# One core, attention block and experts: the output projection between queries and keys, attention's sums in two halves, and three smaller moves

## What is computed

```python
def _L0_attn_ref(q_x, ...):                      # H = 16 heads of HD = 16
    xn = _ln(q_x, ln1_w, ln1_b)
    q = (xn @ wq + bq).reshape(b, n, H, HD).transpose(0, 2, 1, 3)          # k and v likewise
    fq = jax.nn.elu(q) + 1.0
    fk = jax.nn.elu(k) + 1.0
    kv = jnp.einsum('bhnd,bhne->bnde', fk, v)    # a sum over the heads of each token
    qkv = jnp.einsum('bhnd,bnde->bhne', fq, kv)
    k_sum = fk.sum(axis=1)
    qk = jnp.einsum('bhnd,bnd->bhn', fq, k_sum)
    attn = qkv / (qk[..., None] + 1e-06)
    attn = attn.transpose(0, 2, 1, 3).reshape(b, n, c)
    attn = attn @ wo + bo
    x = q_x + attn
    h = _ln(x, ln2_w, ln2_b)
    h = jax.nn.gelu(h @ fc_w + fc_b, approximate=False)
    return x + (h @ proj_w + proj_b)
def _L0_ffn_ref(x, ...):                         # the best K = 2 of 8 experts per sequence
    pooled = x.mean(axis=1)
    logits = pooled @ gate_w.T + gate_b
    ...
    expert_out = jax.nn.gelu(jnp.einsum('bsd,eod->beso', x, expert_w) + expert_b[None, :, None, :], approximate=False)
    return jnp.einsum('be,beso->bso', gates, expert_out)
x = x + _L0_attn_ref(_layernorm(x, axis=-1), ...)
x = x + _L0_ffn_ref(_layernorm(x, axis=-1), ...)
```

## Time and profile before

| | us |
|---|---|
| median of 3 runs | 1235.26 (1235.08 to 1236.95) |
| profiled execution, its own time | 1239.31 |
| its span, first to last instruction | 1237.5 |
| TensorE busy | 1073.0, 87% of the span |
| VectorE busy | 772.0, 62% |
| ScalarE busy | 528.7, 43% |
| GpSimd busy | 190.0, 15% |
| mean granted TensorE clock | 0.907 of full |

### The profile page before, as it was taken

The page is one execution under the profiler, slowest core; times in us unless marked ns, Lnnn a source line. Parts: engine busy times, 40 slices in busy tenths (PEclk is TensorE's granted clock), DMA queues, the critical chain, the costliest instruction groups (busy, mean ns, idle before and its releaser), DMA issues.

```text
span 1237.5 us, 21621 instructions
## 1 busy us (share of the span) xinstructions
PE 1073.0 (87%) x7112; PEld 792.3 (64%) x7112; DVE 772.0 (62%) x1692; ACT 528.7 (43%) x835; POOL 190.0 (15%) x113
## 2 busy tenths in 40 slices
...
DMA packets 242509, 170.06 MB, mean 137 GB/s; under 512 B 177040, under 2 KB 218256, under 8 KB 240144
## 3 DMA queue, kind: packets, MB, share of 16 engines
...
...
## 4 chain that ended last, share of the span: by engine, by line
PE 56%; DVE 16%; issue 9%; DMA 9%; ACT 7%; SPq 1%; POOL 1%; DVEq 1%; ACTq 0%; POOLq 0%
PE pq L963 13%; PE pj L949 10%; PE ps L926 9%; PE pq L871 7%; PE pt L935 5%; DMA nd<-scratch_nd 4%; DMA scratch_nd<-ot 4%; DVE nd L728 3%; DVE am L701 3%; PE pq L908 2%; DVE acc L819 2%; PE ps L1006 2%; PE ps L908 2%; PE pj L1052 2%; PE pt L908 1%
## 5 line engine op out<-in xcount | busy, mean ns | idle before, releaser
L717 DVE TENSOR_TENSOR hidden<-xhT,hidden 128x512 fp32r<-128x512 f32 x128 | 104.0, 812 | 215.2 <-ACT hidden L542 215.1
L541 ACT ACTIVATE xhT<-pq,col 128x512 f32<-128x512 f32 x128 | 88.0, 688 | 333.2 <-PE pq L963 332.9
L963 PE MATMUL pq<-hT,w_fc 128*128 128x512 f32 x768 | 220.3, 426 | 4.9 <-issue 3.1
L949 PE MATMUL pj<-w_pj,hidden 128*128 128x256 f32 x1536 | 213.4, 288 | 2.7 <-DVE hidden L717 2.7
L949 PEld LDWEIGHTS pj<-w_pj,hidden 128*128 128x128 f32 x1536 | 190.8, 188 | 17.3 <-DVE hidden L717 3.7
L926 PE MATMUL ps<-kq 48*128 48x128 f32 x1024 | 155.2, 434 | 35.1 <-DVE am L701 18.5
L926 PEld LDWEIGHTS ps<-kq 48*128 48x128 f32 x1024 | 133.8, 329 | 76.2 <-issue 47.6
L701 DVE TENSOR_TENSOR am<-ps,mask 128x512 f32<-128x512 f32 x256 | 163.9, 681 | 22.3 <-PE ps L926 21.5
L963 PEld LDWEIGHTS pq<-hT,w_fc 128*128 128x128 f32 x768 | 146.6, 204 | 35.2 <-issue 4.8
L871 PE MATMUL pq<-zT,w_e 128*128 (+1 forms) x256 | 116.8, 605 | 9.6 <-DMA b_e<-in_eb 7.3
L458 POOL TENSOR_TENSOR rs<-var,mhalf 128x4 f32<-128x4 f32 x16 | 18.5, 1159 | 559.3 <-DVE var L745 559.3
...
## 6 DMA issues: line engine op xcount, KB each, us to landing
...
scratch_q<-hidden SPq DMA_DIRECT2D x32, 512.0 KB, 4.6
scratch_k<-hidden SPq DMA_DIRECT2D x32, 512.0 KB, 6.1
scratch_nd<-ot SPq DMA_DIRECT2D x16, 1024.0 KB, 3.9
...
x_sb<-in_x SPq DMA_DIRECT2D x16, 512.0 KB, 4.7
scratch_v<-feat_v ACTq DMA_DIRECT2D x16, 512.0 KB, 2.8
```

Source lines behind the costliest of these rows:

```text
L541: nc.scalar.activation(gelub[:, u], pq[u][:, :], ACT.Gelu, bias=b_fc[:, m:m + 1])
L717: nc.vector.tensor_tensor(hidden[:, m % SLOTS, 1], gelub[:, u], hidden[:, m % SLOTS, 0].bitcast(f32), ALU.subtract).then_inc(S["rest_ready ...
L949: last = nc.tensor.matmul(pj[u][:, D * s:D * (s + 1)], hidden[:, m % SLOTS, a, lo:lo + P], w_pj[:, b, m], start=(m == 0 and n == 0 and s = ...
L963: last = nc.tensor.matmul(pq[m % 2][:, :], w_fc[:, b, c, P * m:P * (m + 1)], hT[:, a, c], start=(n == 0), stop=(n == len(order) - 1))
```

## The change

1. **D2 is split.** D2 now holds v and q, and the new stage **D4** holds k. The order is `D2, A2, R, D4, K1, F1, F3, ...` instead of `D2, K1, A2, F1, R, F3, ...`. q goes into the `pt` banks, k into the `pq` banks that held v (`qk_bank`). Rounding of q and k is no longer interleaved with the exponentials. R writes its result to `xhat`, since `hn` holds k's features then.
2. **Sums in two halves.** SyncE stores and reloads the first 64 of each 128 tokens' sums in M2, and the other 64 in M4. VectorE divides the first half in the new stage **N0** after M4, the second in N.
3. **F2 before B9** on TensorE, with the addition in the new stage **FA** behind B9, and **F4 before B0** on VectorE.
4. **GpSimd**: Y's two adds move to **YB** behind JA, R's add to **SA** behind F4.

The diff, cut to its core:

```diff
-FULL = [..., "M3", "Z", "D1", "M4", "XL", "X", "J7", "JA", "E", "VT", "N", "D2", "K1", "A2",
-        "F1", "R", "F3", "B0", "F4", "H", "FX", "B9", "F2"]
+FULL = [..., "M3", "Z", "D1", "M4", "N0", "XL", "X", "J7", "JA", "YB", "E", "VT", "N", "D2", "A2",
+        "R", "D4", "K1", "F1", "F3", "F4", "SA", "B0", "H", "FX", "F2", "B9", "FA"]
...
         def qk_bank(j):
-            return (ps[j], f"ps_full{j}") if j < NC else (pt[j - NC], f"pt_full{j - NC}")
+            return (pt[j], f"pt_full{j}") if j < NC else (pq[j - NC], f"pq_full{j - NC}")
...
-                if p.stage in ("B4", "M4"):
+                if p.stage in ("B2", "M2", "B4", "M4"):
+                    half = int(p.stage[1]) // 2 - 1
+                    part = slice(HALF * half, HALF * (half + 1))
                     wait("pt_free0", at("pt_free0"))
                     wait("pt_free1", at("pt_free1", 1))
-                    sp.dma_start(nd_dram.rearrange("j e h t -> (j e) (h t)"), ot[:, :, :].rearrange("p h t -> p (h t)")
-                                 ).then_inc(S["nd_out"], 16)
+                    sp.dma_start(nd_dram.rearrange("j e h t -> (j e) h t")[:, :, part], ot[:, :, part]).then_inc(S["nd_out"], 16)
                     wait("attnT_ready", at("attnT_ready"))
                     wait("nd_out", at("nd_out", 16))
                     for c, dst in ((0, num[:, 0]), (1, num[:, 1]), (2, den)):
                         src = nd_dram[:, P // H * c:P // H * (c + 1)].rearrange("j e h t -> (e h) j t")
-                        sp.dma_start(dst.rearrange("p (j t) -> p j t", j=NQ), src).then_inc(S["num_in"], 16)
+                        sp.dma_start(dst.rearrange("p (j t) -> p j t", j=NQ)[:, :, part], src[:, :, part]).then_inc(S[f"num_in{half}"], 16)
...
-                if p.stage == "Y":
-                    wait("y_ready", at("y_ready", 1))
+                if p.stage == "YB":
+                    wait("y_ready", at("y_ready"))
+                    for u in range(2):
+                        wait(f"pj_free{u}", at(f"pj_free{u}"))
                     nc.gpsimd.tensor_tensor(x1[:, :, :], x1[:, :, :], rows_of(0), ALU.add).then_inc(S["yb_ready"], 1)
...
-                if p.stage == "R":
+                if p.stage == "SA":
                     slot = x_sb[:, p.t % XRING]
-                    wait("h_ready", at("h_ready", 1))
+                    wait("h_ready", at("h_ready"))
+                    wait("acc_ready", at("acc_ready"))
...
-                if p.stage == "D2":
+                if p.stage in ("D2", "D4"):
+                    lo = 0 if p.stage == "D2" else NC
+                    for j in range(lo, lo + NC):
...
+                def divided(half):
+                    def part(tile):
+                        return tile.rearrange("p c (j b t) -> p c j b t", j=NQ, b=2)[:, :, :, half]
+                    d = part(nd[:, NC:NC + 1])[:, 0]
+                    wait(f"num_in{half}", at(f"num_in{half}"))
+                    link(nc.vector.reciprocal(d, d))
+                    for c in range(NC):
+                        n = part(num)[:, c]
+                        last = nc.vector.tensor_tensor(n, n, d, ALU.mult)
+                    link(last)
+                if p.stage == "N0":
+                    divided(0)
                 if p.stage == "N":
-                    wait("num_in", at("num_in"))
-                    link(nc.vector.reciprocal(den, den))
-                    link(nc.vector.tensor_tensor(num, num, den.unsqueeze(1).broadcast_to([P, NC, T]), ALU.mult))
+                    divided(1)
                     link(nc.vector.tensor_copy(attnT[:, 0], num))
...
-                    normed(hn, x1, lambda s: mv[:, s, 0:1], lambda s: rs[:, s:s + 1]).then_inc(S["h_ready"], 1)
+                    normed(xhat, x1, lambda s: mv[:, s, 0:1], lambda s: rs[:, s:s + 1]).then_inc(S["h_ready"], 1)
...
-                    for j in (4, 5, 0, 1, 2, 3):
+                if p.stage in ("D2", "D4"):
+                    for j in (4, 5, 0, 1) if p.stage == "D2" else (2, 3):
```

More of the change, by code:

```diff
@@ L157, in loop @@
         base = plus(at, rate, hi - lo)
-    first = ["L", "DS", "D1", "X", "D2"]
+    first = ["L", "DS", "D1", "X", "D2", "D4"]
     second = ["K0", "K1", "VL", "VT", "B0", "B9"]
     late = ["XS", "J2", "Z", "E"]
-    last = ["XL", "F1", "F3", "F4", "FX", "F2"]
+    last = ["XL", "F1", "F3", "F4", "FX", "F2", "FA"]
     def without(names, *out):
@@ L349, in run @@
                     sp.dma_start(out_sb[:, :, :], x2_dram[p.t]).then_inc(S["x2_in"], 16)
-                if p.stage == "D2":
-                    for n, c in enumerate("qk"):
-                        for m in range(NC):
-                            wait("lo_ready", at("lo_ready", NC * n + m + 1))
-                            sp.dma_start(qk_dram[n][p.t % 2].rearrange("w u (c p) t -> c p (w u) t", p=P)[m],
-                                         hidden[:, NC * n + m].bitcast(f32).rearrange("p w (u t) -> p (w u) t", t=HALF)
-                                         ).then_inc(S[f"{c}_out"], 16)
+                if p.stage in ("D2", "D4"):
+                    n, c = (0, "q") if p.stage == "D2" else (1, "k")
+                    for m in range(NC):
+                        wait("lo_ready", at("lo_ready", m + 1))
+                        sp.dma_start(qk_dram[n][p.t % 2].rearrange("w u (c p) t -> c p (w u) t", p=P)[m],
+                                     hidden[:, NC * n + m].bitcast(f32).rearrange("p w (u t) -> p (w u) t", t=HALF)
+                                     ).then_inc(S[f"{c}_out"], 16)
                 if p.stage == "VL":
@@ L502, in run @@
                     wait("am_used", at("am_used"))
[L504 to L509 removed]
+                if p.stage in ("D2", "D4"):
+                    lo = 0 if p.stage == "D2" else NC
+                    for j in range(lo, lo + NC):
                         bank, full = qk_bank(j)
                         wait(full, at(full, 1))
[L512 removed]
+                        wait("f_ready", at("f_ready"))
                         nc.scalar.activation(expb[:, j % 2], bank[:, :], ACT.Exp, bias=b_qkv[:, j:j + 1])
@@ L515, in run @@
                                              bias=b_qkv[:, j:j + 1]).then_inc(S[full.replace("full", "free")], 1)
-                        if j:
-                            rounded(j - 1)
-                    rounded(2 * NC - 1)
+                    for j in range(lo, lo + NC):
+                        wait("f_ready", at("f_ready", j - lo + 1))
+                        nc.scalar.activation(hidden[:, j, 0], (fq, fk)[j // NC][:, j % NC], ACT.Identity).then_inc(S["hi_ready"], 1)
                 if p.stage == "VT":
@@ L679, in run @@
                         nc.vector.tensor_tensor(w[:, 1], w32, w[:, 0].bitcast(f32), ALU.subtract).then_inc(split_done, 1)
-                if p.stage == "D2":
-                    def rest(j):
-                        wait("hi_ready", at("hi_ready", j + 1))
-                        src = (fq, fk)[j // NC][:, j % NC]
-                        nc.vector.tensor_tensor(hidden[:, j, 1], src, hidden[:, j, 0].bitcast(f32),
-                                                ALU.subtract).then_inc(S["lo_ready"], 1)
-                    for j in range(2 * NC):
+                if p.stage in ("D2", "D4"):
+                    lo = 0 if p.stage == "D2" else NC
+                    for j in range(lo, lo + NC):
                         _, full = qk_bank(j)
```

73 lines of the change are left out of this document (35 added, 38 removed).

## The result

Before 1235.17 us (1233.54 to 1236.95, 4 runs), changed 1270.88 us (1266.98 to 1275.95, 4 runs): ratio 1.0292, 95% interval 1.026 to 1.0325. The profiled executions took 1239.31 and 1268.08 us (spans 1237.5 and 1266.3), 28.8 us apart. What follows explains the 28.8. The forecast, 1241.0 us, was 30 us too low, and the time lies outside its range.

The account below looks back on a forecast made before the run. It took TensorE's own work to set the pace in iterations with experts, with idle time at the ends and half-clock stretches. Terms 9.6 + 5.7 + 0 - 6.5 - 3 = +5.8 us on the median 1235.26 gave 1241.0; range 1225 to 1255.

Parts of the forecast that it names:

- When A2 can start: Output projection in full iterations: YB's adds delay N's products, so TensorE idles 1.3 us before A2, bounds 0 to 2.5.
- The halves' 2.1 us: VectorE's N: with half the sums divided early, the remaining reciprocal and products are shorter, 2.1 us saved.
- The transfers gain nothing: Stores and reloads of sums: halves land at the same time as before, bounds 1.5 us earlier and 1 us later.
- The experts behind the keys: Between F1 and F3: F3 starts 9.65 us after A2's end, leaving TensorE idle 2.75 us; before it was 0.26.
- What is saved behind F3: F3 to M1 in full iterations takes 8.45 us without waits; net +1.6 us each, +9.6 in six.
- HEAD iterations: The three iterations with gates: the gates' work gives N time to finish for A2; +1.9 us each, +5.7 together.
- Iterations 2 to 6: Iterations without experts: k fills the time behind A2 but K1's data is late; 0 for five, bounds -1.9 to +2 each.
- The end: Iterations 16 and 17: A2 starts earlier and F2's wait for GpSimd goes; together -6.5 us, bounds -3 to -10.
- The clock: TensorE's clock may stay high around second scores but fall during F3; -3 us for both, range -17 to +20.
- The rule weighed: GpSimd adds hold VectorE instructions with two SBUF sources; by the skill's rule one-source ones could be held too.
- rival 4: Slower by more: A2 1.7 us later in 11 iterations, 1259; or clock falls before every F3, 1256. Chance 0.1 together.
- rivals, 2: Faster: the clock stays at 2.4 GHz into M1 and the gap before F3 does not lower it; 1226 us, chance 0.2.

Follow-up runs that it names:

- e13: The changed kernel with D4 and K1 put ahead of A2 again, nothing else; 1207.04 us, ratio 0.9791.
- e10: The kernel of e6 with N0 right ahead of N, so both halves are divided together; 1196.47 us, ratio 0.9698.
- e14: The changed kernel with R put behind D4 and K1, A2 still ahead of k; 1225.47 us, ratio 0.9934.
- e5: The changed kernel with YB's adds back right behind Y and SA's add also waiting for k's rests; 1247.64 us, ratio 1.012.
- e7: The kernel of e5 with R put behind D4 and K1, A2 still ahead of k; 1200.14 us, ratio 0.9723.
- e12: The kernel of e6 with YB behind JA, where the change has it; 1207.99 us, ratio 0.9788.
- e6: The kernel of e5 with D4 and K1 put ahead of A2 again; 1197.46 us, ratio 0.9701.
- e4: The kernel before with YB's two GpSimd adds alone moved behind JA; 1239.49 us, ratio 1.0037.
- e3: The changed kernel with SA's GpSimd add also waiting for k's rests, which changes only iterations 2 to 6; 1260.76 us, ratio 1.0204.

## Why the prediction was wrong

By e13 the change splits in two. The move of the output projection costs +0.3 at the start, +13.7 in 3 to 6, +16.6 with gates, +30.0 in full iterations, -0.9 at the end: 60 us. Everything else gives -7.1, -4.0, +9.4, -23.1, -6.4: -31 us. I had both signs and neither size.

1. **"When A2 can start."** Right in full iterations: waits of 1.35 to 1.95 us against 1.3, because N's products wait for YB. The halves' 2.1 us are no gain there, since A2's start hangs on GpSimd's end or F3 on its own chain (read from the rows; e10 shows it only where k covers N). At the end the early division gave 1.0 and 0.5. "The transfers gain nothing" was wrong, and item 5 has the price.
2. **"The experts behind the keys."** Right in every step: F3 at E + 9.4 instead of E + 9.65, idle 2.38 instead of 2.75. With R behind k's roundings the wait falls to 1.23 (e14; from 3.44 to 1.24 between e5 and e7), so R's place makes half to two thirds of it. Full iterations lose 14.0 us more in e14 than in e13, 13.5 of it idle time.
3. **"What is saved behind F3."** F4, H and F2 run without a wait, as said. F3 to M1 took 902.95 - 893.44 = 9.5 us, not 8.45: F3 itself 1.9 more, at half clock, and F2 0.6 less, at the full one. The forecast net of +9.6 with the clock's -3 is +6.6; measured +6.9. This is luck, agreement of a sum and not of its terms. Over the six iterations the part behind the mark Q grew by 16.5 us, not 12.3, and the part ahead of it shrank by 9.6, not 2.7. Without the move the other edits save 23.1 us there (11.5 less idle time, half-clock time 35.4 to 2.2 us, worth at most 16.6), and the move takes 30.0 (idle 20.2, half clock 16.4 us, worth at most 8.2).
4. **"HEAD iterations", +1.9 each: the step that failed.** Measured 11.5, 7.6 and 6.9, 26.0 instead of 5.7, which is most of the miss. Counted by the mark Q, the part ahead of it, which I took to shrink by 0.2 each, grew by 8.3, 3.0 and 3.3 us; the part behind it grew by 3.2, 4.7 and 3.6, not 2.1. I let the gates' work cover YB and N, and did not ask what YB stands in front of: the copies pb<-gs. TensorE waits 4.28, 4.28 and 3.88 us for them instead of 1.7, and is at half clock for 6.8 us around that in each, where before has 3.4, 3.4 and nothing. e12 against e6 prices this at 7.0, e13 against before at 9.4 with the rest of the change. In i = 7 another 5.0 us are lost ahead of the gates, in M1 to M3: K1's data is late by 1.96, a mask by 0.99, and the clock falls to half twice for 3.4 us. Most of that goes with k's late place in iteration 6: from M1 to the gates' wait it is 39.4 us in before and in e6, 40.9 in e13, and 44.4 here. No run tests it by itself. Behind Q the gap before F3 is 3.6 us, and F3 takes 5.37 for 3.67 in i = 11 and 15, not in i = 7. A2 starts without a wait, and the additions, behind q's rests on VectorE, end at 748.08 in i = 11, E + 1.8 instead of E + 0.7; F3 starts at E + 10.5.
5. **"Iterations 2 to 6", 0:** M1 of iteration 6 came 2.9 us later, inside the bounds, but by another way. The start gave 6.8, for which I had no term. It is the halves: in iteration 2 N waits for the transfer, and the reciprocal starts 8.0 us behind the store's issue instead of 10.9, is 1.6 us shorter and the product 0.5; the store itself is issued 2.0 us sooner. No run takes the halves back alone, but all kernels with them reach this M1 at 124.0 to 128.4 us, and before and e4 at 133.4 and 132.2. SyncE's stores and VectorE's reciprocals, before and changed:

```profile
100.31 0.35 SPq L386 DMA_DIRECT2D scratch_nd<-ot  x1
111.20 3.35 DVE L728 RECIPROCAL nd<-nd 128x512 f32<-128x512 f32 x1 [13.00 <-DMA nd<-scratch_nd]
```

```profile
98.33 0.56 SPq L388 DMA_DIRECT2D scratch_nd<-ot  x1
106.35 1.75 DVE L730 RECIPROCAL nd<-nd 128x256 f32<-128x256 f32 x1 [6.64 <-DMA nd<-scratch_nd]
```

   Then 3 to 6 lost 9.7, of which SA's hold is 7.3 (e3). I had moved SA behind F4 in thought everywhere; without experts there is no F4. K1's wait was there as forecast, 1.1 to 2.0 us against 2.3. (The terms 7.7, 6.5, 8.3 and 3.9 of that forecast add up to E + 26.4, not 26.2.)
6. **"The end", -6.5:** -7.3. The waits were 7.76 and 8.63 us instead of 9.56 and 10.19. YB holds 2.1 and 1.7 of them (e12 against e6), so this too could have been more.
7. **"The clock", -3, from -17 to +20.** Half-clock time fell from 35.4 to 18.6 us in full iterations and from 61 to 54 in 3 to 6, and rose from 20 to 42 us in those with gates. By half of each, the most that it can be worth, that is -8.4, -3.4 and +11: near the -3, again as a sum. e6, e13 and e14 have next to none of it in full iterations.
8. **The rule weighed**, that of the Trainium skill, GPSIMD Engine Reference, Specifications: VectorE instructions in a 2-port mode collide with GpSimd too, not only those with two SBUF inputs. By the earlier trace rows alone only two-source ones are held. The traces agree with the page that one-source ones can be: the pair of copies takes 2.50 us for 0.36, and scalar instructions 1.40 and 2.39. No trace shows the mode that an instruction ran in. The reciprocal, which I named as the likely victim in rival 4, keeps 1.75 us beside YB's add.

Of the rivals, 2 (the clock stays high into M1) and the second half of 4 (it falls before F3) both came true, in the same full iterations, and the first gave back about twice what the second took. Rival 4's first half did not come true, and its 1256 and 1259 us are below the measured time too: no case of mine had a loss at the gates.
